# Attention's row maxima and loads sent in another order by SyncE, and the row scatter in groups of eight

## The reference

```python
def reference(...):
    x = L0_attn_x
    x = _layernorm(x + _L0_attn_ref(x, ...), axis=-1)
    x = _layernorm(x + _L0_ffn_ref(x, ...), axis=-1)
    x = _layernorm(x + _L1_attn_ref(x, ...), axis=-1)
    x = _layernorm(x + _L1_ffn_ref(x, ...), axis=-1)
    return x

def _L0_ffn_ref(...):                      # 16 experts, 2 for each token
    ...
    gate = jnp.zeros((T, E), x.dtype).at[jnp.arange(T)[:, None], idx].add(vals)
    def step(y, p):
        w1, b1, w2, b2, w3, b3, ge = p
        h = jax.nn.silu(xt @ w1 + b1) * (xt @ w2 + b2)
        return (y + ge[:, None] * (h @ w3 + b3), None)
    ...
    z = jax.nn.silu(xt @ sw1 + sb1) * (xt @ sw2 + sb2) @ sw3 + sb3
    return (y + z).reshape(shape)

def _L1_attn_ref(x, w_q, w_k, w_v, w_o):   # 32 heads of 16, batch 4
    ...
    scores = jnp.einsum('bhqd,bhkd->bhqk', q, k) / jnp.sqrt(jnp.float32(D_K))
    attn = jax.nn.softmax(scores, axis=-1)
    out = jnp.einsum('bhqk,bhkd->bhqd', attn, v)
    ...
```

## Time and profile before

| | us |
|---|---|
| median of 3 runs | 1897.57 |
| lowest, highest | 1895.38, 1898.67 |
| the profiled execution, by its clock | 1894.86 |
| the span in its trace | 1892.9 |
| TensorE busy | 1717.8 (91%) |
| VectorE busy | 1463.7 (77%) |
| ScalarE busy | 817.5 (43%) |
| GpSimd busy | 680.8 (36%) |

### The profile page before, as it was taken

One profiled execution on the slowest core, in us unless ns is written; L12 is line 12 of the kernel. 1 busy time (PEld: TensorE's weight loads), 2 busy tenths in 40 slices (PEclk: granted clock), 3 DMA queues, 4 the chain that ended last, 5 costly groups with the idle time before them and its releaser, 6 DMA issues. The chain is left out here.

```text
span 1892.9 us, 24149 instructions
## 1 busy us (share of the span) xinstructions
PE 1717.8 (91%) x7666; PEld 1057.0 (56%) x7666; DVE 1463.7 (77%) x2715; ACT 817.5 (43%) x1415; POOL 680.8 (36%) x419
## 2 busy tenths in 40 slices
PE   7889979777959996999899999998989999999997
PEld 2333324224647874786433333335768878778786
DVE  7999999999826665854589998994866776776677
ACT  6657474444302554331477777776521111111112
POOL 5898999996152654400130000000040230231100
PEclk8999999999979998899999999999989999999999
DMA  6334333321146998764643333320010000000002
GB/s 162 118 120 129 119 120 120 100 84 38 31 172 250 409 414 309 251 237 169 189 127 98 96 96 97 97 66 3 1 67 1 34 34 1 34 34 1 1 1 89
DMA packets 116701, 213.78 MB, mean 113 GB/s; under 512 B 20035, under 2 KB 41923, under 8 KB 115673
## 3 DMA queue, kind: packets, MB, share of 16 engines
q1 hardware_dynamic: 111457, 195.47, 31.0%
q0 software_dynamic: 5120, 16.78, 2.6%
HBM read 148.94 MB, written 63.24 MB: 112 GB/s over the span
## 5 line engine op out<-in xcount | busy, mean ns | idle before, releaser
L2203 DVE TENSOR_REDUCE early_top<-att_first 128x1 f32<-128x512 f32 x480 | 303.3, 683 | 42.4 <-PE att_first L2082 42.4
L562 DVE TENSOR_TENSOR_SCAN ssm_h<-ssm_da,ssm_dbx 128x512 f32<-128x512 f32 x256 | 303.8, 1206 | 1.8 <-ACT ssm_da L441 1.5
L283 POOL TENSOR_TENSOR ssm_dbx<-ssm_u,ssm_bbc 128x2048 f32<-128x2048 f32 x63 | 285.6, 4533 | 26.8 <-DVE ssm_h L562 26.3
L2164 ACT ACTIVATE att_prob<-att_second 128x1024 f32<-128x1024 f32 x256 | 248.1, 1024 | 94.3 <-PE att_second L2103 92.9
L653 PE MATMUL ssm_y<-ssm_hc,all_ident 128*128 128x512 f32 x384 | 214.9, 643 | 44.5 <-DVE ssm_hc L528 44.5
L441 ACT ACTIVATE ssm_da<-ssm_dt,ssm_minus_a 128x512 f32<-128x512 f32 x256 | 176.6, 690 | 168.7 <-DVE ssm_h L562 168.5
L2593 ACT ACTIVATE ffn_silu<-ffn_pg 128x256 f32<-128x256 f32 x112 | 43.2, 386 | 406.5 <-PE ffn_pg L129 406.5
L2458 POOL TENSOR_TENSOR pairs_raw<-pairs_raw,pairs_scales 128x512 f32<-128x512 f32 x42 | 42.3, 1043 | 456.6 <-DMA pairs_raw<-in_w 456.6
L127 PE MATMUL ffn_pg<-pairs_wh,last_XH 128*128 128x512 f32 x448 | 176.5, 394 | 1.7 <-PEq L2256 1.7
L128 PE MATMUL ffn_pg<-pairs_wl,last_XH 128*128 128x512 f32 x448 | 176.6, 394 | 0.0
L129 PE MATMUL ffn_pg<-pairs_wh,last_XL 128*128 128x512 f32 x448 | 175.6, 392 | 0.0
(11 more groups left out here) (356 smaller groups left out, 3725.0 us busy)
## 6 DMA issues: line engine op xcount, KB each, us to landing
all_X<-in_w SPq DMA_DIRECT2D x29, 769.0 KB, 11.3
ssm_bbc<-brow_dram SPq DMA_DIRECT2D x64, 256.0 KB, 4.2
ssm_cbs<-crow_dram SPq DMA_DIRECT2D x64, 256.0 KB, 3.4
sorted_x<-ssm_zero SPq DMA_DIRECT2D x47, 256.0 KB
sorted_y<-exp_y SPq DMA_DIRECT2D x47, 256.0 KB, 11.6
mlps_raw<-in_w SPq DMA_DIRECT2D x14, 769.0 KB, 10.3
pairs_raw<-in_w SPq DMA_DIRECT2D x7, 1536.0 KB, 6.3
v_dram<-all_sums SPq DMA_DIRECT2D x16, 512.0 KB
```

Of the source, the lines that this page charges most:

```text
L283: nc.gpsimd.tensor_tensor(dbx[:, n % 2], u[:, n // STATE % 2], bbc[:, n % RING, :].unsqueeze(1).to_broadcast([P, KC, NB]), ALU.mult).then_ ...
L562: nc.vector.tensor_tensor_scan(h[:, n % 2, c, :], da[:, i % 2, :], dbx[:, n % 2, c, :], 0.0, ALU.mult, ALU.add).then_inc(h_ready, 1)
L2164: nc.scalar.activation(prob[step % 2][:, js, :], p_second[second_place(step, pair) % 2][:], ACT.Exp, scale=DK ** -0.5).then_inc(exp_done, 1)
L2203: nc.vector.tensor_reduce(top[w % 2][:, qt, item:item + 1], p_first[first_place(m) % FIRSTS][:], AX.X, ALU.max).then_inc(max_done, 1)
```

## The change

It has two parts.

*The scatter.* GpSimd now waits, ahead of the tiles 4, 8 and 12 (`PER_BLOCK` is 4), until all scatters issued so far have landed.

*The maxima and loads.* `normalise_and_project` no longer spreads the maxima of set 1; `attend` does so, right after the first v load. Its loop begins at set 1 and loads set s+3 (`LOADED` is 3), not s+4, behind the maxima of set s+1. So set 4's loads move from behind the maxima of no set to behind those of set 2, set 5's from behind set 2's to behind set 3's, and so on. v of set 2, the selection rows and the output weights move behind the first turn of the loop, and the weights of the MLP behind attention (`first_loads`) from ahead of the maxima of set 3 to ahead of those of set 4.

```diff
--- before.py
+++ after.py
@@ -1004,6 +1004,8 @@
 
             pool.wait_ge(placed, 1)
             for t in range(TILES):
+                if t and t % PER_BLOCK == 0:
+                    pool.wait_ge(scattered, 16 * TOP * t)
                 for k in range(TOP):
                     nc.gpsimd.indirect_dma_start(g.sorted_x, bass.IndirectOffsetOnAxis(g.at[:, k, t:t + 1], 0),
                                                  g.X[:, t, :], None).then_inc(scattered, 16)
@@ -1611,10 +1613,6 @@
                 sp.wait_ge(rows_ready, w + 1)
                 store_row_maxima(sp, g, w, f.rows[w], f.rows_out)
 
-            def spread_maxima(w):
-                sp.wait_ge(f.rows_out, 16 * (w + 1))
-                load_row_maxima(sp, g, f.qs[w], w, f.rows_in[w])
-
             for k in (Q, K):
                 if k == K:
 
@@ -1632,8 +1630,9 @@
                     load_select(sp, g, f.ks[u - 26], f.selected)
                 if u - 1 in ROWS_UNIT:
                     send_maxima(ROWS_UNIT.index(u - 1))
-                if u - 2 in ROWS_UNIT:
-                    spread_maxima(ROWS_UNIT.index(u - 2))
+                if u - 2 == ROWS_UNIT[0]:
+                    sp.wait_ge(f.rows_out, 16)
+                    load_row_maxima(sp, g, f.qs[0], 0, f.rows_in[0])
                 if u == 42:
                     sp.wait_ge(product, 1 + max(n for n, unit in enumerate(units) if unit[0] == V))
                     sp.wait_ge(stored[1], 32 * (KC // 2 + 1))
@@ -1653,8 +1652,6 @@
                     sp.dma_start(g.qk_dram[kind - Q, 1, b * KC + c], lo[:, i % 2, :].bitcast(F32)).then_inc(stored[i % 2], 16)
             if ROWS_UNIT[1] + 1 >= len(units):
                 send_maxima(1)
-            if ROWS_UNIT[1] + 2 >= len(units):
-                spread_maxima(1)
 
         @block.gpsimd
         def _(pool):
@@ -2029,24 +2026,27 @@
                 sp.wait_ge(f.v_stored[k], 16 * TILES // 2)
                 sp.wait_ge(f.stored[k], 32 * UNITS)
             load_v(sp, 0)
+            sp.wait_ge(f.rows_out, 32)
+            load_row_maxima(sp, g, f.qs[1], 1, f.rows_in[1])
             load(sp, f.LOADED)
             load_rest(sp, f.LOADED)
-            for w in range(1, f.LOADED):
-                load_v(sp, w)
-            for slot in range(f.LOADED, RING):
-                load_select(sp, g, ks[slot], selected)
-            g.pair_weights.load_wo(sp)
-            for s in range(SETS):
-                if s == 2:
+            load_v(sp, 1)
+            for s in range(1, SETS):
+                if s == 3:
                     g.pair_weights.first_loads(sp)
-                if EARLY_SETS <= s + 1 < SETS:
+                if s + 1 < SETS:
                     send_max(sp, s + 1)
-                if s + RING - 1 < SETS:
-                    load(sp, s + RING - 1)
-                if EARLY_SETS <= s + 1 < SETS:
+                if s + f.LOADED < SETS:
+                    load(sp, s + f.LOADED)
+                if s + 1 < SETS:
                     load_max(sp, s + 1)
-                if s + RING - 1 < SETS:
-                    load_rest(sp, s + RING - 1)
+                if s + f.LOADED < SETS:
+                    load_rest(sp, s + f.LOADED)
+                if s == 1:
+                    load_v(sp, 2)
+                    for slot in range(f.LOADED, RING):
+                        load_select(sp, g, ks[slot], selected)
+                    g.pair_weights.load_wo(sp)
 
         @block.gpsimd
         def _(pool):
```

## The result

| | median, us | range, us |
|---|---|---|
| before | 1898.12 | 1895.38 to 1901.26 (4 runs) |
| changed | 1971.09 | 1968.79 to 1973.57 (4 runs) |

A forecast was written before the change was run, and what follows sets the result against it. It took the scatter to be bound by a 24 us stall and attention by TensorE's own products. 1894.9 + 59.1 (loop) + 14 (clock) - 2.4 (opening) - 17 (scatter) = 1948.6, so 1950 us, range 1924 to 1988.

The forecast's parts named there:

- Scatter: Row scatter in groups of eight: each pause clears the 24 us stall, so the expert stage starts earlier; -17 us.
- the shorter barrier: End of the projection: four maxima DMAs leave it and the barrier, so attention starts up to 1.4 us earlier.
- The rival in which the stall stays: Row scatter: the stall hangs on the traffic, not on how much is queued; 1970 us, chance 0.28.
- The loop: Attention, sets 2 to 29: late q and k loads close a loop of 14.08 us a set; +59.1 us.
- The forecast's sign of 13.7 to 14.5 us a set: Attention in the new trace: time from a set's first product to the next set's first product.
- The clock: Attention: TensorE's idling lowers its granted clock, 1.0 us a fall, half of the possible falls taken; +14 us.
- the sum of 1948.6: Whole kernel: 1894.9 us plus all forecast terms, before 1 to 2 us for the median.
- The opening: Attention's start: waits of 2.84 and 1.66 us for maxima go, set 4's loads are late next; -2.4 us.
- the rule of the loop: Attention: last k load starts 6.76 us behind the store (7.16 in the mean) and lands 2.2 us after issue.
- The late v, select and output-weight loads: Attention: these moved loads are wanted later than they land even so; no cost.
- The faster rival: Attention: the twelve loads are in time, under 7.02 us from store to twelfth landing; 1871 us, chance 0.09.

The follow-up runs named there:

- e9: Kernel before, with three 128x512 fills on GpSimd as a pause after each eight scatters, without waiting for them to land: 1876.58 us (0.9875).
- e8: Kernel before, with one wait in the row scatter, after sixteen scatters: 1889.69 us (0.9949).
- e3: Changed kernel, but set 4 loaded ahead of the loop and set s+4 loaded again in turn s: 1882.97 us (0.9919).
- e4: Changed kernel, with set s+3's q, k and v loads ahead of the wait for set s+1's maxima: 1879.75 us (0.9895).
- e6: Changed kernel, with the four loads of the maxima behind the k and v loads instead of ahead: 2032.39 us (1.0705).
- e7: Changed kernel, with each set's v load issued ahead of its six k loads, not behind: 2005.92 us (1.0558).
- e10: e4's kernel with the last MLP's first 1.5 MB of weights loaded in turn 29, not turn 3: 1871.11 us (0.9856).
- e11: Kernel before, with the scatter in groups of eight and the first 1.5 MB of MLP weights loaded in turn 29, not 2: 1878.76 us (0.9876).
- e1: Kernel before, with the three waits in the row scatter alone: 1880.65 us (0.9901).
- e2: Changed kernel, with the scatter as before, without the three waits: 1993.23 us (1.0505).

## Why the prediction held, and where its sum was off

- **Scatter, forecast -17, measured -19.** From the first scatter to attention's start it is 20.6 us less, of which 1.6 belong to the shorter barrier below. That the pauses clear the stall was right; that the stall hangs on how many scatters are queued was a description without a cause. e9 shows that gaps are what counts, e8 that one is too few, and why stays open. Each pause cost 1.72 us (2.99 less 1.27), not 1.45. The rival in which the stall stays fell, though its 1970 us is the measured time: that number is luck, it came out by other terms.
- **The loop, forecast +59.1 without the clock.** Mechanism and place were right (L2082, a DMA from `qk_dram`, 28 waits of 2.1 us in the median). Store to next first product: 7.16+2.2 = 9.36 forecast, 9.40 measured. e3, e4, e6 and e7 show each link of it. The forecast's sign of 13.7 to 14.5 us a set was missed (15.45), by the clock.
- **The clock, forecast +14, measured +34.** This is the term that was mis-sized. Forecast was 1.0 us for each fall, in half of the sets. The stretch was slowed in 21 of 28 sets, by 1.2 us in most and by 2.4 to 2.6 us in 7 of them, not by 1.0: (5.37-4.12) x 27 = 34. The price of one fall was read from a single set of before, which had been slow for part of the stretch only; the row with the full price (products of 0.79 us, as in the barrier's wake) was not used. Against the trace the sum of 1948.6 was 24.0 us low: 20 are this term, 3 the loop, 3.5 the opening and 1.1 the rest behind set 29, less 2 for the scatter and 1.6 for the time ahead of it. That half of the sets would be slowed was a choice between none and all, without a row for it.
- **The opening, forecast -2.4, measured +1.1.** TensorE's idle time ahead of attention's first product went from 3.88 to 2.29 us, 1.6 less, as forecast. But in the changed kernel TensorE ran at the lower clock for about twice as long as before (to 913, where before it was to 925, the stage's start being at 897 and 919), and set 2's maxima were turned 20.5 us after attention's start, not 17.0. From the store to set 2's first product it took 9.16 us, by the rule of the loop. The forecast put no clock on this stretch.
- **The late v, select and output-weight loads at nothing:** right, the only wait for one of them is of 0.22 us, for v at 901.10. The 1.5 MB for the next stage, one set later, were costed at nothing too. Moving them away gave some 8 us in e4's order (e10), but only 2 in the old order (e11 against e1), within the spread of e11's runs; what they cost in the changed kernel was not isolated.
- **The faster rival** needed 7.02 us from store to the twelfth landing. The shortest in 28 sets was 8.9 us.

## What to carry to other kernels

A list of DMAs behind a wait is at least as late as that wait: when loads are moved by one turn, compute from the waiting instruction to the last landing and hold it against the moment of first use, and then ask whether the work between that use and the wait closes a loop. Let nothing stand between a store and its reload, issue the bulk loads ahead of the wait for it, so that they are through when it comes, and keep megabytes for a later stage away from it (e4 and e10). When TensorE is made to idle in each turn, price the work behind each idle at its lower clock level, from a stretch that was slow from end to end.

## What was not expected of the hardware

- Thirty-two indirect DMAs issued without a gap over 40 us held up the other three compute engines for 24 us at a DMA share of only 0.54, and in that time no load landed on the instruction queues. A gap of 1.9 us after each eight was enough. Missing instructions are not shown to be the cause: in the traces of before, e2 and e8 the engines go on before the next such load. What the scatters take from the other engines, their DMA traffic or GpSimd's own work of issuing them, no run separates.
- Waits of 2 us in most sets of 15 us brought TensorE's granted clock to 0.85 over attention; filling the waits with work lifted it to 0.94 only.
- A 16 KB store was seen 1.4 us after its issue when nothing stood ahead of it (e10), and 7.7 us after it behind 1.5 MB of weights and thirteen smaller loads.
